# A Trainium2 kernel of four attention and four feed-forward layers: LayerNorm statistics in the tails, a change to the rotary and the last attention, and rounding moved between two stages

## The reference

```python
def _layernorm(x, axis=-1, eps=1e-05):
    m = jnp.mean(x, axis=axis, keepdims=True)
    v = jnp.var(x, axis=axis, keepdims=True)
    return (x - m) / jnp.sqrt(v + eps)
```

## Time and profile before

| | |
|---|---|
| median of 3 runs | 3103.66 us (3102.98 to 3105.22) |
| the profiled execution: time / span | 3096.28 us / 3094.5 us |
| busy in the span: PE / DVE / ACT / POOL | 2861.9 / 1972.3 / 1386.0 / 1318.5 us |
| stage a0, 0 to 905 us: PE busy | 858.4 us |
| f0, 905 to 989 | 59.4 |
| a1, 989 to 1183 | 163.3 |
| a2's front, 1183 to 1345, and its heads, 1345 to 1858 | 124.8 and 498.6 |
| f2, 1858 to 2077 | 204.5 |
| a3, 2077 to 2981 | 881.4 |
| f3, 2981 to 3094.5 | 71.5 |

### The profile page before, as it was taken

How to read it: one execution, slowest core, us unless ns; L and a number is a source line. 1 busy time by engine, 2 the same in 40 slices (tenths; PEclk the granted TensorE clock), 3 DMA queues, 4 the chain that set the end, 5 groups by cost and what they waited for, 6 DMA issues and landing times. The chain is left out here.

```text
span 3094.5 us, 44830 instructions
## 1 busy us (share of the span) xinstructions
PE 2861.9 (92%) x16417; PEld 2482.4 (80%) x16452; DVE 1972.3 (64%) x3494; ACT 1386.0 (45%) x3409; POOL 1318.5 (43%) x1177
## 2 busy tenths in 40 slices
PE   7999999999977896789999998989999999999967
PEld 6888888888765784678888886878999999999945
DVE  5777777778764787779888874344444444444453
ACT  3656556566531673234444432214444344443520
POOL 6455445545421754365555530013434444443430
PEclk9999999999987898999999999999999999999988
DMA  4122112212121002111111103100101000000000
GB/s 133 49 58 60 58 51 61 61 50 65 43 83 40 18 5 69 31 45 45 42 38 39 38 16 125 43 22 21 28 21 28 25 24 25 25 28 19 17 28 28
DMA packets 77816, 131.86 MB, mean 43 GB/s; under 512 B 10016, under 2 KB 23584, under 8 KB 77216
## 3 DMA queue, kind: packets, MB, share of 16 engines
q1 hardware_dynamic: 68096, 112.09, 12.2%
q10 hardware_dynamic: 9504, 16.91, 1.7%
HBM read 114.23 MB, written 14.75 MB: 42 GB/s over the span
## 5 line engine op out<-in xcount | busy, mean ns | idle before, releaser
L89 PE MATMUL a_pa<-a_wo,a_ot 128*128 128x512 f32 x2304 | 538.5, 391 | 10.3 <-issue 7.5
L89 PEld LDWEIGHTS a_pa<-a_wo,a_ot 128*128 128x128 f32 x2304 | 429.7, 188 | 105.9 <-issue 13.1
L362 DVE SCALAR_TENSOR_TENSOR a_nf_acc<-a_nf_t,a_nf_acc 128x512 f32<-128x512 bf16 (+1 forms) x462 | 403.1, 873 | 42.4 <-ACT a_nf_t L316 11.4
L316 ACT ACTIVATE a_nf_t<-a_nf_w,a_nf_shifts 128x512 bf16<-128x512 f32 (+1 forms) x495 | 321.7, 709 | 204.0 <-DVE a_nf_w L346 174.4
L89 PE MATMUL a_pa<-h_t,a_wqk 128*128 128x512 f32 x1536 | 373.1, 395 | 1.7 <-DVE h_t L773 1.7
L89 PEld LDWEIGHTS a_pa<-h_t,a_wqk 128*128 128x128 f32 x1536 | 281.8, 188 | 56.4 <-DVE h_t L773 1.9
L89 PE MATMUL a_pa<-a_wv,ctx_t 128*128 128x512 f32 x960 | 233.0, 399 | 29.1 <-POOL a_wv L532 15.5
L89 PE MATMUL a_pa<-ctx_t,a_wqk 128*128 128x512 f32 x960 | 226.8, 393 | 21.5 <-POOL a_wqk L1651 21.2
L89 PEld LDWEIGHTS a_pa<-a_wv,ctx_t 128*128 128x128 f32 x960 | 180.6, 191 | 66.8 <-issue 15.5
L89 PEld LDWEIGHTS a_pa<-ctx_t,a_wqk 128*128 128x128 f32 x960 | 181.2, 189 | 60.8 <-POOL a_wqk L1651 23.2
L1009 POOL TENSOR_TENSOR a_prob<-a_prob,a_inv 128x512 f32<-128x512 f32 x128 | 130.6, 1042 | 182.5 <-DVE a_inv L1375 182.5
(11 more groups left out here) (360 smaller groups left out, 5979.2 us busy)
## 6 DMA issues: line engine op xcount, KB each, us to landing
a_raw<-in_a_w SPq DMA_DIRECT2D x288, 256.0 KB, 2.6
a_nf_w<-in_nf ACTq DMA_DIRECT2D x32, 256.0 KB, 2.7
nf_rounded<-a_nf_acc ACTq DMA_DIRECT2D x32, 256.0 KB, 2.0
f_rows<-nf_rounded SPq DMA_DIRECT2D x22, 256.0 KB, 3.0
ctx_kept<-ctx_t SPq DMA_DIRECT2D x1, 4096.0 KB, 17.1
ctx_t<-ctx_kept SPq DMA_DIRECT2D x1, 4096.0 KB, 14.6
f_cols<-nf_rounded SPq DMA_DIRECT2D x11, 256.0 KB, 3.7
a_ctx_raw<-in_ctxt SPq DMA_DIRECT2D x4, 512.0 KB, 6.3
```

What stands on the lines that cost most here:

```text
L89: ins = nc.tensor.matmul(out, lhs(a), rhs(b), start=first and i == 0, stop=last and i == 2)
L316: self.nc.scalar.activation(self.t[:, m % NF4_RING, cols], self.w[:, p % 2, cols], ACT.Identity, bias=self.shifts[:, u - 2:u - 1], scale=s ...
L362: ins = nc.vector.scalar_tensor_tensor(acc, t, c, acc, inner, outer)
```

## The change

- `CarriedNorm`: the LayerNorm statistics of f0, a1, f2, a3 and f3 begin in the tail of the stage ahead. After DVE adds the last output of block b to `x`, it takes `bn_stats` of block b-1; after block 4 it also aggregates blocks 0 to 3, and POOL computes their scale. At the start of the new stage block 0 is applied at once, then the statistics of block 7 and the second half follow. In f0, f2 and f3 the applications alternate with the low parts. In f0 and f3 POOL's weight splits wait until the eight blocks are applied.
- Rounding: a0 does 20 pieces and a2 12 and the quarter. In a0 the slots are 23 units per pair of heads. In a2's front 2 units are left of 24, and each head takes 3, 2 and 3. In a2 the two first units of the next piece are done eight units ahead of the end of a piece (`early`).
- a3: ACT writes the squares as two rows of 64 partitions (four instructions for a head in place of two), DVE adds them (`fold_squares`), and PE sums by four matmuls with two output columns each (`sides`). An output product waits for its own half's `o_taken`. In every fourth head `queries(h + 2, 0)` goes ahead of the next head's scores.
- a1: the loads have two semaphores, and the weights of the projections and the first two blocks are split ahead of the output weights.

```diff
+class CarriedNorm(Norm):
+
...
+    def take_on_vector(self, nc, b, x):
+        nc.vector.bn_stats(self.stats[:, b, :], x[:, b, :]).then_inc(self.own, 1)
+
+    def half_on_vector(self, nc, dve, g):
+
+        bs = slice(4 * g, 4 * g + 4)
+        dve.wait_ge(self.own, 8 * g + 4)
+        for b in range(4 * g, 4 * g + 4):
+            nc.vector.bn_aggr(self.mv[:, b, :], self.stats[:, b, :]).then_inc(self.own, 1)
+        dve.wait_ge(self.own, 8 * g + 8)
+        nc.vector.tensor_scalar(self.var[:, bs], self.mv[:, bs, 1], 1e-5, None, ALU.add).then_inc(self.var_ready, 1)
+
+    def half_on_gpsimd(self, nc, pool, g):
+        bs = slice(4 * g, 4 * g + 4)
+        pool.wait_ge(self.half_set, 1)
+        pool.wait_ge(self.var_ready, g + 1)
+        nc.gpsimd.tensor_tensor(self.rstd[:, bs], self.var[:, bs], self.half[:, bs], ALU.pow).then_inc(self.rstd_ready, 1)
...
+        norm.apply(nc, 0, h[:, 0, :], x).then_inc(self.h_ready, 1)
+        norm.take_on_vector(nc, NB - 1, x)
+        norm.half_on_vector(nc, dve, 1)
+        for b in range(1, NB):
+            if b == 4:
+                dve.wait_ge(norm.rstd_ready, 2)
+            norm.apply(nc, b, h[:, b, :], x).then_inc(self.h_ready, 1)
+            if b >= 3:
+                low(b - 3)
+        for b in range(NB - 3, NB):
+            low(b)
...
-SIZES0 = [8] * 24
-SIZES2 = [8] * 8 + [2]
+SIZES0 = [8] * 20
+SIZES2 = [8] * 12 + [2]
 assert sum(SIZES0) + sum(SIZES2) == NF4_BLOCKS
...
+            if not self.early:
+                if n < len(self.sizes) * NF4_UNITS:
+                    yield n // NF4_UNITS, n % NF4_UNITS
+                continue
+            if n < 2:
+                yield 0, n
+                continue
+            p, u = (n - 2) // NF4_UNITS, (n - 2) % NF4_UNITS
+            if u < 8:
+                p, u = p, u + 2
+            elif u < 10:
+                p, u = p + 1, u - 8
+            if p < len(self.sizes):
+                yield p, u
+
     def on_scalar(self, act, count):
...
                 if p > 0:
-                    dve.wait_ge(self.done, p)
+                    dve.wait_ge(self.v_ready, p)
+                if p > 1:
+                    dve.wait_ge(self.done, p - 1)
...
-                        rounding.on_scalar(act, 3 if h % 2 == 0 else 2)
+                        rounding.on_scalar(act, 2 if h % 2 == 0 else 1)
                     keep(("k", h + 2, 1))
...
                 nc.vector.tensor_tensor(x[:, b, :], bank(key), x[:, b, :], ALU.add).then_inc(added, 1)
+                if n == H // 2 - 1 and b > 0:
+                    dve.wait_ge(added, added_count["o", n, b - 1])
+                    ahead.take_on_vector(nc, b - 1, x)
+                    if b == 4:
+                        ahead.half_on_vector(nc, dve, 0)
 
...
                 rest_of_o(h, 1)
-                rounding.on_vector(dve, 10 if h % 2 else 13)
+                rounding.on_vector(dve, 7 if h % 2 else 10)
...
                 out = tile_of(("ss", head))
-                pe.wait_ge(squared, 2 * head + 2)
-                for b in range(NB):
-                    ins = nc.tensor.matmul(out[:, b:b + 1], q2[:, b * P:(b + 1) * P], ones[:, :], start=True, stop=True)
+                pe.wait_ge(folded, head + 1)
+                for i in range(4):
+                    ins = nc.tensor.matmul(out[:, 2 * i:2 * i + 2], q2[:, 0, i * P:(i + 1) * P], sides[:, :],
+                                           start=True, stop=True)
...
             def output(n, b):
+                pe.wait_ge(o_taken, 4 * n + 3 + b // 4)
...
                 transpose_weights(h, 0)
                 transpose_weights(h, 1)
+                if h % 4 == 3 and h + 2 < H:
+                    queries(h + 2, 0)
                 if h + 1 < H:
                     scores(h + 1, 0)
                     scores(h + 1, 1)
-                if h + 2 < H:
+                if h % 4 != 3 and h + 2 < H:
                     queries(h + 2, 0)
...
-                    pe.wait_ge(o_taken, 2 * h + 2)
...
                 act.wait_ge(a_ready, made_count[key])
-                nc.scalar.activation(q2[:, cols], bank(key), ACT.Square).then_inc(squared, 1)
+                for rows in range(2):
+                    nc.scalar.activation(q2[64 * half:64 * half + 64, rows, :], bank(key)[64 * rows:64 * rows + 64, :],
+                                         ACT.Square).then_inc(squared, 1)
...
+            def fold_squares(head):
+                dve.wait_ge(squared, 4 * head + 4)
+                nc.vector.tensor_tensor(q2[:, 0, :], q2[:, 0, :], q2[:, 1, :], ALU.add).then_inc(folded, 1)
...
                 if h + 2 < H:
+                    fold_squares(h + 2)
...
     def side(step):
-        return (2, 1, 2) if step < 14 else (2, 0, 2)
+        return (3, 2, 3)
...
+            rounding.on_scalar(act, 2)
             exps(0, 0)
...
-            rounding.on_vector(dve, 3 * NB)
+            rounding.on_vector(dve, 2)
...
             pool.wait_ge(loaded, 48)
+            pool.wait_ge(norm.h_ready, NB)
             nc.gpsimd.tensor_scalar(base[:, HI, :, :], raw[:, :, :], 1.0, 0.0, ALU.mult, ALU.add).then_inc(base_split, 1)
...
-            for b in range(NB):
-                norm.apply(nc, b, norm_h[:, b, :], x).then_inc(h_ready, 1)
-            for b in range(NB):
+                if group == FF_GROUPS - 1 and b > 0:
+                    dve.wait_ge(d_used, d)
...
+            dve.wait_ge(norm.rstd_ready, 1)
+            for b in range(4):
+                norm.apply(nc, b, norm_h[:, b, :], x).then_inc(h_ready, 1)
+            turn(0, range(3))
+            dve.wait_ge(norm.rstd_ready, 2)
+            for b in range(4, NB):
+                norm.apply(nc, b, norm_h[:, b, :], x).then_inc(h_ready, 1)
+                rest_of_h(b - 4)
+            for b in range(4, NB):
+                rest_of_h(b)
             for n in range(HC2):
                 product(n, 0)
...
             norm.on_gpsimd(pool)
+            pool.wait_ge(norm.h_ready, NB)
```

More of the change, by code:

```diff
@@ L254, with __init__ @@
     SCALE = 2.0 ** 60
-    def __init__(self, nc, st, at, flat_in, rounded, first, sizes):
+    def __init__(self, nc, st, at, flat_in, rounded, first, sizes, early, ring):
         code = np.array(NF4_CODE, np.float32)
@@ L321, in on_vector @@
         nc = self.nc
-        for unit in range(self.dve_at, min(self.dve_at + count, len(self.sizes) * NF4_UNITS)):
-            p, u = unit // NF4_UNITS, unit % NF4_UNITS
+        for p, u in self.units(self.dve_at, count):
             cols, blocks = slice(0, self.width(p)), self.sizes[p]
@@ L2878, in _ @@
         def _(pool):
[L2879 to L2880 removed]
+            norm.half_on_gpsimd(nc, pool, 1)
+            ahead.half_on_gpsimd(nc, pool, 0)
         @block.tensor
```

285 lines of the change are left out of this document (132 added, 153 removed).

## The result

The changed kernel takes 3078.91 us, median of 4 runs (3076.83 to 3084.36), against 3103.32 (3098.11 to 3105.22, also 4). The ratio is 0.9927, 95% interval 0.9908 to 0.9945: 0.7% faster, 24 us. Forecast were 3062 us, 41 us less. The profiled execution took 3076.83 us, its span 3074.7, so 19.8 us less than the span of before.

The account below looks back on a forecast made before the run. PE bounds the large stages a0, a2's heads and a3. -24 - 21 + 44 - 34.9 + 2.7 + 4 - 1.4 - 1.5 - 9 = -41 us, from 3103.66 to 3062 us; range 3028 to 3090.

Parts of the forecast that it names:

- a0: Rounding moved out: ACT's key copy goes earlier, PE's waits and lost clock vanish; -24 us, low end -12, high -27.
- a3: Half as many squares matmuls -29.5 us, scores' waits for keys -4, last output -1.4; the new chain stays hidden.
- f0: Start of the stage: -1.4 us, since PE still waits for the cast behind POOL's splits of 4.60.
- f3: Start: -9 us; -7 if small casts and subtractions are held to POOL's end, -16 if not.
- f2: Statistics: +4 us in its tail, where DVE sets the pace, and -1.5 at its start.
- rival 2: Gains in a0 or a3 fall short: ACT's copies still wait (-12) or squares' addition is late (-16); about 3078, chance 0.16.
- Front of a2: Two units left of 24: 18.9 us of PE's idle go and 2.2 of low clock; -21 us.
- Heads of a2: Eight units a head make DVE the bound: 17.7 us per head against 16.06, +44 us; bounds +9 to +85.
- Rival 1: Heads of a2 absorb the units, +9 to +15 in place of +44; time about 3030, chance 0.16.
- rival 3: Slower: a2's heads lose over 3.15 us each, PE and DVE delaying each other; 3118, chance 0.08 slower, 0.05 equal.
- a1: Start of the stage: 0, since its keys are placed behind POOL's mask, whose DMA lands at 1003.63.
- Its signs: a0 881, a3 870 us; a2 front idle 2 to 3, head 17.7; squares matmuls 115 ns; f3 router at 20 to 22.

Follow-up runs that it names:

- the run with six: Changed kernel with before's pieces and a0 slots, 2 units in a2's front, 6 per head of a2 in place of 8: 3050.6 us, ratio 0.9847.
- the mended kernel: Changed kernel with before's pieces and a0 slots, early units (a0, a2), six per a2 head, values' copies between, f3's casts first, old query order: 3006.84 us, ratio 0.9697.

## Why the prediction was right, and where its steps failed

The direction, the stage that loses and the range were right; the size (-41 forecast, -24 by the medians) was missed by two terms that were too large and three that were too small. a0 and a3 fell short by 34.0 us, and f0, f3 and f2 brought 13.1 more than forecast. That the time lies within the range is in part the luck of this balance. It is nearest to rival 2 (about 3078), whose headline came true for a0 and a3, but not by the ways it named: ACT's copies no longer waited at the pieces' starts, and PE waited only 2.1 us for the addition of the squares.

- *Front of a2* (-21): right. From the stage's start to the first scores it took 134.6 us, 155.3 before: -20.7.
- *Heads of a2* (+44, 17.7 us per head): right, 17.79. DVE's busy time was forecast at 17.1 and was 16.98, its idle time at 0.6 and was 0.8. The closeness is in part luck: the 0.888 us for a term was read from a mean over two forms (0.915 for the full one, then 0.945), and the small shifts of the softmax, two a head, fell from a mean of 0.420 (L1981) to 0.251 us (L2009), for which nothing was reckoned. That PE is the bound with six units and DVE with eight is shown by the run with six. Rival 1 (the heads absorb the units) fell, rival 3 (PE and DVE delay each other) stayed far off its 3.15 us.
- *a0* (-24): the mechanism was right (fewer units ahead of the copy free it), and the run with denser slots gives the size back to a microsecond. The step that failed is the one that wasn't taken: the prediction costed the units of a pair of heads and didn't count how many pairs there are slots for, as it did in a2. 360 units by 23 end in the last two heads, where ACT has only three units a head. This took 12.9 us. The reason given beside it, that DVE would no longer be behind, holds only in part: ACT still waits 76.6 us for the division.
- *a3* (-34.9): the price of the squares' own matmuls was right: with nothing in the way the next ones start 0.81 us after the squares' in place of 1.70, 0.89 us a head or 28.5 in all (29.5 forecast). What failed is the sentence that named only the new chain as what could take it back. PE ran into ACT's copies of the values, which the squares' time had covered: 9.3 us. The new chain itself, which the forecast held to be hidden, cost 4.9; a place where it shows is the stage's start, where PE waits 1.88 us for the addition (L1367), which takes 1.33 us there. For the squares these terms make -14.3, where the run with the squares as before shows -10.5: 3.8 us are not accounted for. The rest of the stage, forecast at -4.7, brings 2.2. The last output gave its 1.2 (from the matmuls behind the last squares' to the stage's end it is 41.2 us in place of 42.4). With 0.7 for the statistics, as forecast and not measured here, that leaves about 1.7 for the changed order in place of 4, with the old squares. Its waits only change their releaser, and in the mended kernel it costs 4.0. What it costs in the changed kernel by itself wasn't tried.
- *f0* (-1.4): too small. The step that failed kept the cast behind POOL's split of 4.60 us. The low parts end 9.8 us after the stage's start, and that split begins at 13.5, so the cast and the subtraction are done before it. Only POOL's first, short split can meet them, and in this execution it came too late even for that; the other traces have f0 6.4 to 7.5 us shorter than before, this one 8.7.
- *f3* (-9, between 7 and 16): -12.3. The forecast lay between casts held to POOL's end (-7) and not held (-16). The casts and subtractions waited for one long instruction of POOL and one short one, not for all four. By the lock rule of the Trainium skill ("SBUF — State Buffer", "Who interferes with whom"), the cast can wait for the instruction that holds the ports and no longer, and the trace agrees: 4.20 us behind an instruction of 4.49, and 0.20 when it comes first. With the casts ahead f3 is 18.8 us shorter than before. The wait of POOL for the eight applications, which the change added here, does nearly nothing (0.6 us): POOL would have waited for its DMA.
- *a1 and f2*: a1 -0.2 (forecast 0), f2 +0.6 (forecast +2.5, of which 4 for the statistics in its tail and -1.5 for its start); which of the two was off isn't shown.
- *Its signs*: a head at 17.79 us and PE's idle of 2.24 us in a2's front came as told. a0 was to take 881 and a3 870 us and took 895.3 and 891.4, and f3's router began after 16.2 us, not 20 to 22. A squares matmul with two columns takes 120 ns (30.6 / 256), a little over the 115 that the prediction named as its limit.

## What to carry to other kernels

Filler work needs slots on both engines for its last unit too: count units against slots to the end of the stage, since an engine that runs out of slots early holds up the other's real work. Before time is taken out of the bounding engine, list everything that the removed time covered, not only the new chain. And if filler makes an engine late, look first at where its dependent steps begin (here the maximum and division of a piece; moving them ahead took a0 from 906.6 to 883.5 us) before moving work into a stage whose margin is two microseconds a head.
